# Softplus in a scan-bound kernel: one logarithm with a bias on ScalarE, the rounding term on VectorE, and new orders for all engines

## The chip, the cores and the metric

The kernel runs on one core of one Trainium2 chip. The metric is device time in microseconds (us). The engines are named as the profile names them: PE is TensorE, DVE is VectorE, ACT is ScalarE, POOL is GpSimd, SP is the engine whose queue issues the DMAs.

## The reference

x has the shape (16, 1024, 256) in fp32: 16 sequences of 1024 steps and 256 features. Two feed-forward blocks stand around a state-space block, each with a layer norm ahead of it:

```python
x = x + 0.5 * ffn(layernorm(x))          # silu(x Wg) * (x Wu), then Wd; hidden width 768
x = x + attn(layernorm(x))
x = x + 0.5 * ffn(layernorm(x))

def attn(x):                             # e = 256 features, n = 16 states
    z, params = x @ W_z.T, x @ W_params.T
    dt = softplus(params[..., :64] @ W_dt.T + b_dt)
    u  = silu(causal_conv(x, conv_w))    # 4 taps, one filter for each feature
    A  = -exp(A_log)
    A_tilde = exp(dt * A)
    B_tilde = where(|A| < 1e-5, dt, (A_tilde - 1) / (A + 1e-10))
    h[t] = A_tilde[t-1] * h[t-1] + B_tilde[t-1] * u[t-1]     # for each feature and state
    y  = sum over n of C[t, n] * h[t, e, n]
    return ((y + u * D) * silu(z)) @ W_out.T
```

The step that is changed is the softplus. It is evaluated as max(y, 0) + log(1 + exp(-|y|)), with a correction for the rounding of the sum: with s = 1 + e rounded to fp32 and v = s - 1, the term e - v that the rounding lost is added back.

## The kernel before, in words

The 16 sequences are called rows. Each row has 1024 steps, in two chunks c of 512, and 256 features, in two halves h (or p) of 128 partitions. For each row there are 32 scans (16 states by two halves), each over 128x1024. For each of them:

- ACT makes the decays with an exponential of dt times a coefficient (event `ex`, L1043),
- DVE scans them into the PSUM tensor g_bank (event `scan`, L1282) and multiplies the result by the inverse coefficient and by the row of C (event `cm`, L1318),
- POOL adds that product to acc (also event `cm`, L1122), and the SP queue fetches the next row of C, spread over the partitions.

The first and the last row are cut the other way: their scans are over 128x512, two to a state (one for each half) and chunk, 64 in the row.

Around the scans, and beside them, run the two feed-forward blocks of the neighbouring rows: PE makes the gate and up products (L782) and the down product (L794), ACT takes silu and scales (L925, L933), POOL or DVE multiplies them (L1090, L1235), DVE takes the layer norm's statistics (L1193, L1201) and the residual (L1243). The events `ai` and `aj` (L1254, L1260) start acc on DVE.

The softplus is made for each half and chunk, four times a row and 64 times in all, on tiles of 128x512:

- `da` on ACT: |y| into dt (L1001), max(y, 0) into sp_r (L1004), exp(-|y|) into dt (L1006);
- `dl` on ACT: sp_l = 1 + dt (L1013), sp_v = sp_l - 1 (L1016, the tile that the profile calls odd), sp_l = ln(sp_l) (L1018), each waiting for the one before;
- `dp` on POOL: sp_l - sp_v (L1077), + dt (L1080), + sp_r into dt (L1082).

The order of all work is written out. The tables ROW (rows in the middle), HEAD (row 0), SECOND (row 1), LATE (row 14) and TAIL (row 15) give each event a time in units of one scan; `schedule()` sorts all events by it, and each engine issues its own part of that one list, in order. Each engine is an in-order queue: an instruction whose semaphore isn't there holds up all behind it. Semaphores are counted ahead by the class Counts from the same list. DVE's program stands twice in the kernel, once for inputs with coefficients below 1e-5 and once without; a branch at its start picks the one, and with these inputs it is the short one (one instruction to a scan).

Of the kernel before, what the change touches and what calls it, by code (L numbers as in the profile page):

```python
# [1355 lines left out]
```

## Time and profile before

| | |
|---|---|
| median of 3 runs | 2221.56 us (2221.4 to 2221.57) |
| the profiled execution | 2221.01 us |
| its span in the trace | 2219.1 us |
| granted TensorE clock, mean over the span | 0.977 |

The profile is of one execution; its span runs from the first to the last instruction, and some 1.9 us of its time lie outside. Engine times in it are the unions of the instructions' own times; register, branch and semaphore work isn't counted. A row of a listing by line gives the engine, the operation, what is written <- what is read, the shapes, the count, then the busy time in us and the mean of one in ns, then the idle time of that engine just before these instructions and who ended it. In a listing in order of time the first number is the start and the second the duration, both in us. In a wait of less than 150 ns no releaser is named.

### The profile page before, as it was taken

What the parts mean: (1) busy time and instruction counts of PE and PEld (TensorE: products, weight loads), DVE (VectorE), ACT (ScalarE), POOL (GpSimd) and SP (SyncE); (2) the same over time, 40 slices, a digit from 0 to 9 for tenths busy, and PEclk for the clock granted to TensorE, in tenths of its full rate; (3) what the DMA queues carried; (4) which work ended last, traced back from release to release, by engine and by line L of the source; (5) the groups of instructions that cost most, each with busy time, mean ns of one, the idle gap of its engine ahead of it and who ended that gap; (6) DMA issues with size and microseconds to landing.
All of it is one profiled execution on the core that took longest, in us unless ns stands there. A gap on an engine that the chain in (4) does not pass through costs nothing. (4 is left out here: it accounts for less than half of the span.)

```text
span 2219.1 us, 27781 instructions
## 1 busy us (share of the span) xinstructions
PE 2110.7 (95%) x8708; PEld 1286.0 (58%) x8708; DVE 2088.8 (94%) x2233; ACT 1961.2 (88%) x2946; POOL 1946.3 (88%) x1510
## 2 busy tenths in 40 slices
PE   6995999999999999999999999999999999998578
PEld 3452656566565656656565665656566565656245
DVE  2599999999999999999999999999999999999992
ACT  5988898989999898999989899998989999896882
POOL 2687899899999989999998999999899999998673
PEclk9997999999999999999999999999999999999779
DMA  2122444444444444434444444444444444433120
GB/s 94 44 82 68 141 136 152 152 144 152 135 154 142 151 153 144 152 135 152 143 148 152 149 151 136 152 138 149 152 149 150 140 152 135 152 134 123 63 71 29
DMA packets 112023, 291.14 MB, mean 131 GB/s; under 512 B 11201, under 2 KB 45314, under 8 KB 111874
## 3 DMA queue, kind: packets, MB, share of 16 engines
q1 hardware_dynamic: 111874, 289.35, 39.5%
q8 instruction: 69, 1.13, 0.2%
q14 instruction: 80, 0.66, 0.1%
HBM read 271.49 MB, written 17.83 MB: 130 GB/s over the span
## 5 line engine op out<-in xcount | busy, mean ns | idle before, releaser
L1282 DVE TENSOR_TENSOR_SCAN g_bank<-du_bank,ring 128x1024 f32<-128x1024 f32 (+1 forms) x512 | 1099.8, 2154 | 9.3 <-ACT ring L1043 2.5
L1122 POOL TENSOR_TENSOR acc<-acc,ring 128x1024 f32<-128x1024 f32 x512 | 1023.5, 1999 | 79.9 <-DVE ring L1318 66.7
L794 PE MATMUL work<-wd_t,hid 128*128 128x256 f32 x3072 | 684.8, 380 | 4.3 <-DVE hid L1235 4.2
L1318 DVE SCALAR_TENSOR_TENSOR ring<-g_bank,inv_a,ring 128x1024 f32<-128x1024 f32 (+1 forms) x576 | 661.5, 1154 | 5.3 <-POOL acc L1122 2.5
L794 PEld LDWEIGHTS work<-wd_t,hid 128*128 128x128 f32 x3072 | 582.3, 190 | 116.0 <-issue 20.1
L1043 ACT ACTIVATE ring<-dt,a_coef 128x1024 f32<-128x1024 f32 (+1 forms) x576 | 578.2, 1048 | 1.8 <-POOL dt L1082 0.2
L1090 POOL TENSOR_TENSOR hid<-hid,odd 128x512 f32<-128x512 f32 x320 | 347.4, 1093 | 69.2 <-ACT hid L933 40.5
L782 PE MATMUL work<-xt_hi,wg_t 128*128 128x512 f16 x768 | 296.1, 386 | 20.7 <-ACT odd L925 6.2
L782 PE MATMUL work<-xt_hi,wu_t 128*128 128x512 f16 x768 | 297.0, 387 | 12.8 <-ACT hid L933 4.5
L925 ACT ACTIVATE odd<-work 128x512 f32<-128x512 f32 x384 | 222.0, 606 | 89.1 <-PE work L782 87.3
L782 PE MATMUL work<-xt_lo,wu_t 128*128 128x512 f16 x768 | 296.4, 386 | 0.0
L782 PE MATMUL work<-xt_lo,wg_t 128*128 128x512 f16 x768 | 295.8, 385 | 0.0
L861 ACT ACT_TABLE_LOAD x213 | 273.3, 1283 | 3.8
L833 PE MATMUL work<-xt,tap_diag 128*128 128x512 f32 x512 | 228.1, 592 | 2.7 <-ACT sp_r L1004 1.4
L933 ACT ACTIVATE hid<-work 128x512 f32<-128x512 f32 x320 | 186.7, 593 | 25.0 <-PE work L782 24.7
L833 PEld LDWEIGHTS work<-xt,tap_diag 128*128 128x128 f32 x512 | 96.7, 189 | 121.7 <-issue 114.9
L782 PEld LDWEIGHTS work<-xt_hi,wg_t 128*128 128x128 f16 x768 | 75.8, 99 | 126.2 <-ACT xt_lo L912 13.1
L782 PEld LDWEIGHTS work<-xt_hi,wu_t 128*128 128x128 f16 x768 | 76.0, 99 | 115.2 <-issue 16.6
L782 PEld LDWEIGHTS work<-xt_lo,wu_t 128*128 128x128 f16 x768 | 76.2, 99 | 94.4 <-issue 22.9
L804 PE MATMUL work<-wo_t,acc 128*128 128x256 f32 x512 | 125.5, 390 | 5.4 <-POOL acc L1113 5.3
L782 PEld LDWEIGHTS work<-xt_lo,wg_t 128*128 128x128 f16 x768 | 76.0, 99 | 94.0 <-issue 18.8
L811 PE MATMUL work<-xt,wz_t 128*128 128x512 f32 x256 | 123.8, 606 | 6.0 <-ACT hid L933 3.3
...
## 6 DMA issues: line engine op xcount, KB each, us to landing
...
```

What stands on the lines that cost most here:

```text
L782: last = pe.matmul(dst[:], w[:, k, m * P:(m + 1) * P], part_[:, k, :], start=(k == 0 and i == 0), stop=(k == EH - 1 and i == 1))
L794: last = pe.matmul(dst[:, j * E:(j + 1) * E], hid[:, K.unit[f, bt, c, m] % HIDS, t:t + P], wd_t[:, m, :], start=(m == 0), stop=(m == HM - 1))
L804: last = pe.matmul(dst[:, j * E:(j + 1) * E], acc[bt % 2][:, h, t:t + P], wo_t[:, h, :], start=(h == 0), stop=(h == EH - 1))
L833: last = pe.matmul(dst[:], tap_diag[:, h, k, :], xt[:, h, k + c * CH:k + (c + 1) * CH], start=(k == 0), stop=(k == KW - 1))
L861: nc.scalar.preload_act_table_set(name)
L925: nc.scalar.activation(sil[:, K.at["silu", ev][1] % SILUS, :], bank(job)[:], ACT.Silu, scale=GATE_SCALE).then_inc(freed(job), 1)
L933: nc.scalar.activation(hid[:, K.unit[ev[1:]] % HIDS, :], bank(job)[:], ACT.Copy, scale=H_SCALE).then_inc(freed(job), 1)
L1043: nc.scalar.activation(dst, dt[bt % 2][:, h, t], ACT.Exp, scale=a_coef[:, h, s:s + 1]).then_inc(S["decay"], 1)
L1090: nc.gpsimd.tensor_tensor(v, v, sil[:, k, :], ALU.mult).then_inc(S["product"], 1)
L1122: nc.gpsimd.tensor_tensor(v, v, shaped(bt, cg[:, K.number[ev[1:]] % TERMS, :]), ALU.add).then_inc(S["summed"], 1)
L1282: scan = nc.vector.tensor_tensor_scan(g, du_h, d_h, first[0], ALU.add, ALU.mult)
L1318: nc.vector.scalar_tensor_tensor(v, g, inv_a[:, h, s:s + 1], c_row, ALU.mult, ALU.mult).then_inc(S["weighted"], 1)
```

## The change

ACT's part of `dl` is one instruction in place of three: the logarithm of dt with a per-partition tile of ones as its bias. The rounding term sp_v is made on DVE, by one TENSOR_SCALAR with two additions (+1, then -1), which is a new event on DVE's list with its own semaphore sp_one. POOL's first subtraction waits for both. All five tables of times are new, so the order on every engine is another one.

```diff
 ROW = {
-    "da": [-9.914, -9.105, -4.311, -1.005],
-    "dl": [-9.438, -5.645, -3.692, -0.598],
-    "dp": [-10.06, -4.984, -2.59, -1.097],
+    "da": [-8.362, -8.161, -5.086, -3.146],
+    "dl": [-7.272, -4.465, -2.733, -2.14],
+    "dp": [-7.183, -4.139, -2.053, -1.976],
...
-            return [(one[kind], {"da": 2, "dp": 3, "dl": 3, "Ts": EH}.get(kind, 1))]
+            more = [("sp_one", 1)] if kind == "dl" else []
+            return more + [(one[kind], {"da": 2, "dp": 3, "Ts": EH}.get(kind, 1))]
...
                     wait(act, "sp_exp", ("da", bt, h, c))
                     wait(act, "sp_sum", ("dp", bt, h - 1, c) if h else ("dp", bt - 1, EH - 1, c))
-                    nc.scalar.activation(sp_l[:, c, :], dt[bt % 2][:, h, 1 + c * CH:1 + (c + 1) * CH], ACT.Copy,
-                                         bias=1.0).then_inc(S["sp_ln"], 1)
-                    wait(act, "sp_ln", ev, less=2)
-                    nc.scalar.activation(sp_v[:, c, :], sp_l[:, c, :], ACT.Copy, bias=-1.0).then_inc(S["sp_ln"], 1)
-                    wait(act, "sp_ln", ev, less=1)
-                    nc.scalar.activation(sp_l[:, c, :], sp_l[:, c, :], ACT.Ln).then_inc(S["sp_ln"], 1)
+                    nc.scalar.activation(sp_l[:, c, :], dt[bt % 2][:, h, 1 + c * CH:1 + (c + 1) * CH], ACT.Ln,
+                                         bias=ones[:]).then_inc(S["sp_ln"], 1)
...
                     wait(pool, "sp_ln", ("dl", bt, h, c))
+                    wait(pool, "sp_one", ("dl", bt, h, c))
                     nc.gpsimd.tensor_tensor(sp_l[:, c, :], sp_l[:, c, :], sp_v[:, c, :],
                                             ALU.subtract).then_inc(S["sp_sum"], 1)
...
+                    elif kind == "dl":
+
+                        _, bt, h, c = ev
+                        wait(dve, "sp_exp", ("da", bt, h, c))
+                        wait(dve, "sp_sum", ("dp", bt, h - 1, c) if h else ("dp", bt - 1, EH - 1, c))
+                        nc.vector.tensor_scalar(sp_v[:, c, :], dt[bt % 2][:, h, 1 + c * CH:1 + (c + 1) * CH], 1.0, -1.0,
+                                                ALU.add, ALU.add).then_inc(S["sp_one"], 1)
```

The order shows how DVE's list moves. The first piece is of DVE before, in the last third of a middle row; L1282 is a scan (the listing writes it as SCALAR_TENSOR_TENSOR into g_bank), L1318 the product with C that needs it, and the square brackets name the semaphores that an instruction waits for.

```order
L1282 SCALAR_TENSOR_TENSOR g_bank<-du_bank,ring 128x1024 [waits decay,weighted]
L1254 TENSOR_TENSOR work<-work,u 128x512 [waits u_first,bank_ready0]
L1318 SCALAR_TENSOR_TENSOR ring<-g_bank,inv_a,ring 128x1024 [waits summed,c_spread0,scanned]
L1254 TENSOR_TENSOR work<-work,u 128x512 [waits bank_ready2]
L1282 SCALAR_TENSOR_TENSOR g_bank<-du_bank,ring 128x1024 [waits decay,weighted]
L1260 SCALAR_TENSOR_TENSOR acc<-u,consts,work 128x512 [waits times_u]
L1260 SCALAR_TENSOR_TENSOR acc<-u,consts,work 128x512
L1318 SCALAR_TENSOR_TENSOR ring<-g_bank,inv_a,ring 128x1024 [waits summed,c_spread1,scanned]
L1243 SCALAR_TENSOR_TENSOR x_fin<-work,x_fin 128x512 [waits bank_ready3]
```

The second piece is of DVE after the change, at the same place. The lines have moved: L1290 is the scan, L1326 the product, L1262 the new TENSOR_SCALAR, L1268 the old L1260 and L1244 the old L1243.

```order
L1326 SCALAR_TENSOR_TENSOR ring<-g_bank,inv_a,ring 128x1024 [waits summed,c_spread1,scanned]
L1262 TENSOR_SCALAR odd<-dt 128x512 [waits sp_sum,sp_exp]
L1290 SCALAR_TENSOR_TENSOR g_bank<-du_bank,ring 128x1024 [waits decay,weighted]
L1268 SCALAR_TENSOR_TENSOR acc<-u,consts,work 128x512 [waits times_u]
L1326 SCALAR_TENSOR_TENSOR ring<-g_bank,inv_a,ring 128x1024 [waits summed,c_spread2,scanned]
L1290 SCALAR_TENSOR_TENSOR g_bank<-du_bank,ring 128x1024 [waits decay,weighted]
L1244 SCALAR_TENSOR_TENSOR x_fin<-work,x_fin 128x512 [waits bank_ready0]
L1326 SCALAR_TENSOR_TENSOR ring<-g_bank,inv_a,ring 128x1024 [waits summed,c_spread0,scanned]
L1290 SCALAR_TENSOR_TENSOR g_bank<-du_bank,ring 128x1024 [waits decay,weighted]
L1262 TENSOR_SCALAR odd<-dt 128x512 [waits sp_sum,sp_exp]
L1326 SCALAR_TENSOR_TENSOR ring<-g_bank,inv_a,ring 128x1024 [waits summed,c_spread1,scanned]
```

A middle row now has four L1262 among its 32 scans, each alone between a scan and a product: three behind a scan, one behind a product. The pairs with nothing between them change too: in a middle row before, 5 scans are followed at once by their own product and 14 products at once by the next scan; after, 3 and 11.

On ACT the three instructions of `dl` become one. The first piece is of ACT before, in a middle row (L1043 makes decays):

```order
L1001 ACTIVATE dt<-work 128x512
L1004 ACTIVATE sp_r<-work 128x512
L1006 ACTIVATE dt<-dt 128x512
L1043 ACTIVATE ring<-dt,a_coef 128x1024 x2
L1013 ACTIVATE sp_l<-dt 128x512
L1016 ACTIVATE odd<-sp_l 128x512
L1018 ACTIVATE sp_l<-sp_l 128x512
```

The second is of ACT after, in a middle row (L1005, L1008, L1010 are the old L1001, L1004, L1006; L1017 is the logarithm with its bias):

```order
L1005 ACTIVATE dt<-work 128x512
L1008 ACTIVATE sp_r<-work 128x512
L1010 ACTIVATE dt<-dt 128x512
L1043 ACTIVATE ring<-dt,a_coef 128x1024
L1017 ACTIVATE sp_l<-dt,consts 128x512
```

Over the whole program ACT's list falls from 214 table loads (L861, now L865) to 184.

## Rows read from the trace of the kernel before

**Rows 1.** Part 1 of the page: busy us, share of the span, instructions.

```profile
PE 2110.7 (95%) x8708; PEld 1286.0 (58%) x8708; DVE 2088.8 (94%) x2233; ACT 1961.2 (88%) x2946; POOL 1946.3 (88%) x1510
```

**Rows 2.** Busy time by stretch, cut at rows' first scans (columns: its first line).

```profile
core 0: us, PE busy (x) PEld busy (x) DVE busy (x) ACT busy (x) POOL busy (x), PEclk, DMA share, GB/s
0.00:82.94 82.94, 65.01 (x263) 36.88 (x264) 18.29 (x71) 56.01 (x99) 30.02 (x41) 1.00 0.23 73
82.94:222.12 139.18, 109.39 (x365) 56.12 (x365) 133.15 (x198) 123.97 (x198) 109.88 (x83) 0.90 0.23 71
...
354.13:1910.94 1556.81, 1552.01 (x6530) 956.59 (x6528) 1548.92 (x1538) 1431.76 (x2137) 1457.69 (x1129) 1.00 0.44 147
...
2039.00:2166.64 127.64, 83.78 (x295) 47.63 (x296) 121.96 (x170) 105.07 (x149) 90.01 (x61) 0.76 0.23 70
2166.64:2219.10 52.46, 44.66 (x207) 30.28 (x205) 9.69 (x20) 15.06 (x27) 18.62 (x17) 0.99 0.09 31
```

**Rows 3.** DVE by line, rows 2 to 13: busy us, mean ns, idle before.

```profile
L1282 DVE TENSOR_TENSOR_SCAN g_bank<-du_bank,ring 128x1024 f32<-128x1024 f32 x385 | 880.9, 2288 | 5.8
L1318 DVE SCALAR_TENSOR_TENSOR ring<-g_bank,inv_a,ring 128x1024 f32<-128x1024 f32 x384 | 488.9, 1273 | 2.1
L1193 DVE BATCH_NORM_STATS2 stats<-x_mid 128x6 f32<-128x256 f32 x96 | 39.2, 408 | 0.0
...
L1243 DVE SCALAR_TENSOR_TENSOR x_fin<-work,x_fin 128x512 f32<-128x512 f32 x49 | 33.2, 677 | 0.0
...
L1201 DVE BATCH_NORM_AGGREGATE meanvar<-stats 128x2 f32<-128x6 f32 x288 | 26.4, 155 | 0.0
```

**Rows 4.** DVE in order of time, row 7: start us, duration us.

```profile
1002.77 2.29 DVE L1282 TENSOR_TENSOR_SCAN g_bank<-du_bank,ring 128x1024 f32<-128x1024 f32 x1
1005.09 1.28 DVE L1318 SCALAR_TENSOR_TENSOR ring<-g_bank,inv_a,ring 128x1024 f32<-128x1024 f32 x1
1006.41 2.30 DVE L1282 TENSOR_TENSOR_SCAN g_bank<-du_bank,ring 128x1024 f32<-128x1024 f32 x1
...
1016.05 1.29 DVE L1318 SCALAR_TENSOR_TENSOR ring<-g_bank,inv_a,ring 128x1024 f32<-128x1024 f32 x1
1017.25 0.68 DVE L1235 SCALAR_TENSOR_TENSOR hid<-odd,work 128x512 f32<-128x512 f32 x1
1017.85 2.29 DVE L1282 TENSOR_TENSOR_SCAN g_bank<-du_bank,ring 128x1024 f32<-128x1024 f32 x1
1020.05 0.40 DVE L1193 BATCH_NORM_STATS2 stats<-x_fin 128x6 f32<-128x256 f32 x1
1020.36 1.27 DVE L1318 SCALAR_TENSOR_TENSOR ring<-g_bank,inv_a,ring 128x1024 f32<-128x1024 f32 x1
```

**Rows 5.** DVE's smallest SBUF-to-SBUF groups, whole span.

```profile
L1171 DVE TENSOR_SCALAR part_ident<-ident 128x128 f16<-128x128 f32 x1 | 0.2, 226 | 0.0
...
L1162 DVE TENSOR_SCALAR kept<-tiny 128x32 f32<-128x32 f32 x1 | 0.2, 182 | 0.0
```

**Rows 6.** POOL's groups by line, rows 2 to 13.

```profile
L1122 POOL TENSOR_TENSOR acc<-acc,ring 128x1024 f32<-128x1024 f32 x385 | 769.6, 1999 | 52.4 <-DVE ring L1318 43.1 <-POOL acc L1122 0.9
L1090 POOL TENSOR_TENSOR hid<-hid,odd 128x512 f32<-128x512 f32 x240 | 260.8, 1093 | 10.5 <-ACT hid L933 10.5
...
L1080 POOL TENSOR_TENSOR odd<-sp_l,dt 128x512 f32<-128x512 f32 x48 | 52.5, 1095 | 3.8
...
L1113 POOL TENSOR_TENSOR acc<-acc,odd 128x1024 f32<-128x1024 f32 x24 | 48.0, 1999 | 0.0
```

**Rows 7.** Two of ACT's groups by line, whole span.

```profile
L861 ACT ACT_TABLE_LOAD x213 | 273.3, 1283 | 3.8
...
L1016 ACT ACTIVATE odd<-sp_l 128x512 f32<-128x512 f32 x64 | 40.4, 632 | 2.0
```

**Rows 8.** All engines in order of time, before the first scan.

```profile
77.53 0.63 ACT L1018 ACTIVATE sp_l<-sp_l 128x512 f32<-128x512 f32 x1
...
82.94 1.23 DVE L1282 TENSOR_TENSOR_SCAN g_bank<-du_bank,ring 128x512 f32<-128x512 f32 x1 [0.21 <-ACT ring L1043]
```

More of the change, by code:

```diff
@@ L153 @@
-    "op": [35.06, 36.163, 37.79, 39.377],
-    "rc": [35.575, 36.637, 36.528, 37.925],
-    "ra": [36.686, 37.081, 38.723, 40.428],
[62 rows of a table added]
+    "gate": [22.902, 33.832],
+    "scan": [2.069, 2.861, 3.745, 5.331, 6.972, 8.54, 8.917, 9.446, 10.237, 11.213, 12.305, 13.392, 14.705, 16.607,
+        17.327, 19.066, 19.869, 20.405, 21.329, 21.6, 22.847, 23.595, 24.545, 25.735, 27.009, 27.752, 28.449, 29.234,
+        29.829, 30.713, 32.618, 33.544],
+    "cm": [2.475, 3.732, 5.293, 6.006, 7.925, 8.789, 9.081, 9.751, 10.367, 11.766, 12.502, 14.578, 15.507, 16.878,
+        18.1, 19.134, 20.165, 20.818, 21.522, 22.324, 23.034, 24.127, 25.71, 25.972, 27.116, 28.088, 28.829, 29.566,
+        29.96, 31.503, 32.904, 33.713],
@@ L210 @@
[L210 to L215 removed]
+    "sj1": [-416.545, -399.359, -383.731, -309.346, -259.77, -234.766, -224.568, -206.525],
@@ new lines @@
+    "ln1": [-300.165, -152.578],
+    "lr1": [-217.189, -172.147],
+    "lx1": [-263.701, -147.013],
+    "T1": [-216.593, -95.986],
+    "Te1": [-201.163, -132.221],
+    "Ts1": [-214.325, -82.539],
+    "Tl1": [-192.654, -116.794],
+    "sj2": [-97.203, -95.012, -84.414, -81.252, -23.364, -18.874, -17.593, -16.986],
+    "ln2": [-80.219, -14.269],
+    "lr2": [-53.401, -19.383],
+    "lx2": [-66.256, -12.97],
+    "T2": [-53.486, -5.584],
+    "Te2": [-62.765, -8.441],
+    "ga1": [-209.213, -200.065, -137.254, -98.472, -88.211, -70.776, -72.81, -69.074, -61.766, -61.738, -56.328,
+        -28.093],
@@ new lines @@
+    "dn1": [-66.802, -63.76, -19.221, -17.962],
+    "rs1": [-97.511, -81.18, -27.411, -22.036],
+    "rp": [-78.255, -55.327, -25.504, -25.451],
+    "pm": [-51.651, -5.189],
+    "pe": [-55.742, -4.478],
+    "cw": [-28.111, -3.013],
+    "cv": [-34.106, 1.213, -48.635, 11.32],
+    "us": [-40.893, 3.227, -39.643, 8.84],
+    "z": [16.197, 15.329, -0.006, 16.371],
+    "zs": [12.346, 12.848, 6.559, 18.212],
+    "dt": [-49.921, -0.736, -45.552, 7.04],
+    "da": [-54.127, -3.181, -50.793, 7.492],
@@ new lines @@
+    "dl": [-53.514, 1.324, -43.065, 9.226],
+    "dp": [-49.193, 3.092, -46.694, 8.992],
+    "rm": [-26.762, 4.775, -24.47, 8.913],
+    "ai": [-39.579, 11.469, -35.873, 10.39],
+    "aj": [-36.658, 14.18, -35.797, 11.736],
+    "u0": [-38.941],
+    "dt0": [-38.811],
+    "d": [-41.304, 7.587],
+    "db": [-35.737, 10.134],
+    "gate": [16.924, 33.677],
+    "scan": [-34.028, -30.332, -24.192, -21.131, -12.669, -10.607, -8.982, -6.795, -3.112, -0.993, 0.146, 4.081,
+        4.384, 4.747, 9.566, 10.92, 12.484, 14.917, 15.499, 16.491, 18.184, 20.055, 21.029, 23.235, 23.868, 24.26,
+        26.333, 27.657, 28.693, 28.969, 30.9, 31.904],
@@ new lines @@
+    "Te1": [-85.227, -53.861],
+    "Ts1": [-79.389, -47.402],
+    "Tl1": [-83.712, -50.472],
+    "sj2": [-27.454, -26.946, -26.414, -25.609, -16.662, -15.628, -14.263, -14.127],
+    "ln2": [-21.241, -13.942],
+    "lr2": [-20.1, -12.896],
+    "lx2": [-15.908, -12.768],
+    "T2": [-13.71, -12.475],
+    "Te2": [-15.02, -12.368],
+    "ga1": [-65.443, -55.976, -47.669, -44.736, -41.89, -38.591, -37.859, -34.567, -28.964, -28.785, -27.778,
+        -22.995],
+    "si1": [-71.898, -62.691, -45.971, -48.563, -46.118, -40.471, -41.085, -35.479, -27.739, -24.851, -27.354,
+        -24.194],
@@ new lines @@
+    "up1": [-55.972, -52.12, -45.867, -42.011, -40.268, -37.272, -44.768, -37.612, -33.853, -31.404, -27.389,
+        -18.302],
+    "sc1": [-65.911, -60.842, -49.985, -47.625, -42.45, -47.795, -35.317, -30.637, -32.352, -25.151],
+    "hp1": [-53.927, -44.657, -41.52, -45.734, -41.872, -34.431, -38.55, -25.173, -27.452, -24.818],
+    "sh1": [-39.679, -21.305],
+    "dn1": [-33.884, -31.023, -16.297, -13.854],
+    "rs1": [-35.232, -30.827, -19.282, -14.153],
+    "rp": [-32.402, -28.249, -18.083, -16.296],
@@ new lines @@
+    "pm": [-13.575, -11.07],
+    "pe": [-13.76, -8.204],
+    "cw": [-15.275, -14.049],
+    "cv": [-12.48, -9.462, -5.177, -4.642],
+    "us": [-8.831, -9.408, -5.309, -5.111],
+    "z": [1.568, 6.615, 0.066, 12.303],
+    "zs": [0.357, 6.119, -0.65, 12.334],
+    "dt": [-13.438, -8.327, -7.074, -1.522],
+    "da": [-13.283, -7.794, -6.473, -2.315],
+    "dl": [-12.049, -6.23, -4.261, -2.007],
+    "dp": [-11.989, -6.843, -3.678, -1.765],
+    "rm": [0.171, -4.774, 3.791, -4.26],
+    "ai": [-0.729, -2.577, 2.936, -3.055],
@@ L259 @@
+    "aj": [2.286, 1.5, 3.976, -1.148],
+    "u0": [-2.866],
+    "dt0": [0.808],
 }
 LATE = {
[20 rows of a table removed]
[20 rows of a table added]
 }
 TAIL = {
[19 rows of a table removed]
[L304 to L310 removed]
@@ L317 @@
-    "op": [41.513, 43.467, 110.745, 111.473],
-    "rc": [37.192, 43.796, 102.83, 102.955],
-    "ra": [35.129, 39.708, 111.342, 118.198],
[19 rows of a table added]
+    "gate": [25.544, 91.569],
+    "scan": [1.744, 3.381, 3.72, 5.487, 7.128, 8.771, 13.019, 13.293, 16.026, 17.155, 18.293, 20.077, 20.813, 21.526,
+        23.533, 24.464, 26.624, 31.364, 34.81, 36.513, 37.812, 40.294, 48.785, 51.645, 53.921, 54.754, 58.93, 69.693,
+        71.719, 72.998, 75.231, 81.755],
+    "cm": [2.693, 3.644, 4.563, 6.624, 7.923, 10.402, 13.066, 13.941, 17.06, 17.194, 19.526, 20.371, 21.428, 22.665,
+        23.647, 25.035, 29.386, 32.151, 35.331, 37.189, 38.044, 41.408, 51.235, 53.698, 54.099, 56.924, 66.524, 70.2,
+        72.247, 74.739, 81.13, 85.342],
@@ L320 @@
+    "op": [36.631, 38.424, 112.916, 114.857],
+    "rc": [33.937, 35.654, 96.722, 99.356],
+    "ra": [30.166, 30.868, 101.188, 142.773],
 }
```

119 lines of the change are left out of this document (36 added, 83 removed), and 235 rows, old and new, of tables (LATE, ROW, SECOND, TAIL).

## Prediction

> **What bounds the kernel now.** I read the page's busy shares first, then the busy time by stretch, then the groups of the engine that is fullest, then its instructions in order of time.
>
> The shares alone don't decide: PE 95%, DVE 94%, ACT and POOL 88% [rows 1]. The stretches do. Rows 2 to 13 run from 354.13 to 1910.94, 1556.81 us for 12 rows or 129.73 a row, and in them DVE is busy for 1548.92, so idle for 0.66 us a row. PE shows 1552.01, but ends of matmuls are modelled, so that this number can't tell a full PE from a nearly full one. ACT is idle for 125 us (10.4 a row) and POOL for 99 (8.3 a row) [rows 2].
>
> That DVE sets the period can be added up from its own starts. From a scan to the next instruction it is 2.20 us when something independent follows (1017.85 to 1020.05) and 2.32 when its own product follows at once (1002.77 to 1005.09). From a product it is 1.20 to an independent instruction and 1.32 to the next scan. So a pair with nothing in between costs 0.12 more. An instruction of 128x512 that fills a gap takes 0.60 (1017.25 to 1017.85), BN_STATS 0.31 [rows 4]. A group of four aggregates is 26.4/72 = 0.37 busy, some 0.29 once the overlap of 0.08 with its neighbour is off [rows 3]. A middle row before has 32 scans, 32 products, 19 such bare pairs (5 + 14), 24 BN_STATS, 6 groups of aggregates and 16 instructions of 128x512 (four lines like L1243, which the reader sees with 49 in 12 rows [rows 3]):
>
> 32 x 2.20 + 32 x 1.20 + 19 x 0.12 + 24 x 0.31 + 6 x 0.29 + 16 x 0.60 = 108.8 + 2.3 + 7.4 + 1.7 + 9.6 = 129.8 us.
>
> The measured row is 129.73. DVE has nothing left to give; whatever is added to it lengthens the row, and whatever is taken from ACT there shortens nothing.
>
> **The change part by part.**
>
> *ACT loses work.* Two of three instructions go, 64 times each; one takes 0.63 us [rows 7], and 30 of 214 table loads at 1.28 go with the new order [rows 7]: 128 x 0.63 + 30 x 1.28 = 119 us of ACT. The logarithm's bias becomes a tile; no row here shows what that adds, and with 10 us a row idle even half a microsecond for each of four would stay hidden. In the middle rows I cost all of this at nothing, since DVE covers it. At the head it counts once: the last softplus stands in the chain to the first scan (L1018 at 77.53, first scan at 82.94 [rows 8]); ahead of L1018 go two dependent instructions of 0.63 [rows 7], so -1.3 us. The bounds are 0 and -2.6, for two such groups ahead of the first scan.
>
> *DVE gets 64 TENSOR_SCALARs of 128x512.* No such size is in the trace. The nearest rows of that operation are 182 ns for 32 elements and 226 for 128 [rows 5]: 0.46 ns an element, where one element a cycle costs about 1.0 (677 ns for 512, 408 for 256, hence 1.05 [rows 3]). So it streams two a cycle: 182 + 480 x 0.46 = 403 ns, as long as a BN_STATS of 408, and I take that one's 0.31 to 0.32 from start to start. The other bound is one element a cycle, 677 ns and 0.60. Each fills a gap, and a middle row has 14 bare pairs after (3 + 11) for 19 before: 4 x 0.32 - 5 x 0.12 = +0.68 us a row; by the slow bound 4 x 0.60 - 0.6 = +1.8.
>
> *What the new instruction does beside POOL.* This is the term that decides. No instruction of DVE's in the middle rows takes two elements a cycle out of SBUF; those of before run beside POOL and keep their durations to the nanosecond (677, 736, 408 [rows 3]), and so do POOL's (1999, 1093 [rows 6]). The two TENSOR_SCALARs that the trace has ran during the setup, with POOL idle. So the trace bounds it only from both sides: no wait, or a wait until the POOL instruction under way has ended, at most 2.00 us. If DVE and POOL can't run such a pair together, an arrival at any moment finds POOL busy, and the wait that is left is the sum of squares over twice the time: 385 of 1999 ns, 48 of about the same length (L1113 is one of the two groups), 240 of 1093 and five groups of 48 like L1080 [rows 6]: (433 x 4.0 + 480 x 1.2)/(2 x 1556.8) = 0.74 us. For four a row that is 3.0 us.
>
> I take the wait. The double rate has to use something that the single rate doesn't, and the Trainium skill names it. Its page "SBUF — State Buffer", section "Who interferes with whom", says that VectorE and GpSimd share one pair of SBUF ports, that a tensor_scalar in a two-port mode takes it as an exclusive lock, and that whoever comes second is blocked until the first has ended. "VectorE: DVE Perf Modes", section "Mode 2×_2P", gives that mode to an fp32 tensor_scalar from SBUF to SBUF, as the slope of [rows 5] agrees; that it blocks no row of before shows. By the pages the sum is the one with the wait, by the rows of before alone it is anything from none to the whole. Without these sentences the wait stands as a guess between 0 and 2.00 us, at its mean for a random arrival.
>
> Behind the waiting TENSOR_SCALAR stand, in three of four places, a product L1326, and in the fourth a scan; for the product waits POOL's addition, for both waits ACT's next decay. POOL has 8.3 us a row idle, so it pays nothing for being held for 4 x 0.4.
>
> *The sum.* Of 64 TENSOR_SCALARs two stand ahead of the first scan and 62 between the first and the last, 15.5 rows' worth. Span 2219.1, with 1.9 outside 2221.0. Plus 15.5 x 0.68 = 10.5, plus 62 x 0.74 = 45.9, minus 1.3 at the head, minus 2 for row 0, where DVE is idle for 6.0 of 139.18 us [rows 2] and a third of that may take up its share. 2274.1. The median is 0.5 above the profiled run, so 2274 to 2275.
>
> **The rivals.**
>
> *No wait on POOL.* For it: DVE's and POOL's durations are steady today. Against: none of today's pairs is of this kind. Two elements a cycle: 2221.0 + 10.5 - 1.3 = 2230. One a cycle: 2221.0 + 15.5 x 1.8 - 1.3 = 2248.
>
> *Ends that pay for it (the other side).* The orders of row 0 and of the last row are new, and there DVE has room: 82.94 us before the first scan with 18.29 busy, 6.0 idle in row 0, 5.7 of 127.64 in the last row, and 52.46 us behind the last scan [rows 2]. Less ACT work could let those rows run at DVE's pace: -1.3 and one table load of 1.3 at the head, -6.0 and -5.7 in the rows, together -14.3. With the TENSOR_SCALARs at 0.32 and no wait: 2221.0 + 10.5 - 14.3 = 2217. It decides from 10.5 us on and is a gain to be measured from 15. Against it: 129.8 against 129.73 says that 12 rows can't give anything, and behind the last scan PE, with 44.66 busy of 52.46, has as many products left as before.
>
> *A stall on semaphores.* In DVE's in-order list the TENSOR_SCALAR waits for ACT's exponential and, for the second half, for POOL's three additions of the first (3 x 1.09 behind up to 2.00 [rows 6]). Some 15 us of DVE work lie between the two, so I give it little. If each came 0.5 to 1 us early: 2221.0 + 10.5 + 31 to 62 = 2262 to 2294. It would show as idle time before the instruction, the wait on POOL as a long instruction or as idle time without a semaphore.
>
> **How the numbers follow.** The wait on POOL 0.50 (four fixed phases a row, each 0 to 2.0, so their mean scatters: 2255 to 2295 by itself); no such wait 0.26, 2228 to 2248; the stall 0.06; ends that pay and more, 0.11, 2205 to 2217; ends that pay just so, 0.07. Less than 0.2% (4.4 us) can't be told from no change here. So slower 0.82, the same 0.07, faster 0.11. The predicted time is that of the first case, 2274. The range reaches down over the no-wait case to 2224 and up to 2298, where most of the first case ends; every TENSOR_SCALAR waiting for the whole of a long addition would be 2221.0 + 10.5 + 124 = 2355, which I leave out.
>
> **What would show it.** Right: a row of 133.4 us in the middle (129.73 now), DVE still idle for less than 1 us of it apart from what stands before L1262, L1262 with a mean near 1.1 us or with idle time before it, its times spread from 0.4 to 2.4; ACT idle for some 20 us a row, POOL for about 10. The scans at 2288 ns and the products at 1273 as before. Wrong: L1262 at 0.40 or 0.68 without spread, and rows of 130.4 or 131.5. Quite wrong: rows under 129.7, since then DVE didn't set them; or a gain at the ends, to be seen as a first scan before 80 us and less than 50 us behind the last one.

## The result, and the profile after

The changed kernel takes 2247.66 us (median of 3 runs, 2245.72 to 2249.33), where the kernel before takes 2221.56: a ratio of 1.0116, with a 95% interval of 1.0102 to 1.013. It is slower by 26 us; the forecast was 53. The profiled execution took 2247.66 us with a span of 2245.9.

First the page's busy shares, the line that answers to [rows 1]:

```profile
PE 2117.9 (94%) x8708; PEld 1277.0 (57%) x8708; DVE 2126.4 (95%) x2297; ACT 1856.5 (83%) x2788; POOL 1954.7 (87%) x1510
```

DVE has 37.6 us more, ACT 104.7 less, POOL 8.4 more although it runs the same 1510 instructions. Then the busy time by stretch, cut at the rows' first scans as in [rows 2]:

```profile
0.00:76.54 76.54, 58.79 (x230) 31.08 (x230) 19.68 (x74) 50.67 (x89) 28.99 (x40) 0.98 0.25 79
76.54:213.80 137.26, 112.88 (x399) 61.78 (x398) 134.21 (x202) 123.41 (x195) 112.06 (x84) 0.95 0.24 74
346.97:1937.70 1590.73, 1564.29 (x6530) 951.70 (x6529) 1578.77 (x1585) 1353.36 (x2017) 1464.56 (x1129) 1.00 0.43 144
2068.50:2196.20 127.70, 84.70 (x306) 48.78 (x307) 122.75 (x172) 94.64 (x140) 92.28 (x63) 0.79 0.23 70
2196.20:2245.87 49.67, 42.25 (x195) 28.41 (x193) 9.62 (x20) 14.29 (x25) 16.10 (x15) 0.98 0.10 32
```

Against [rows 2], stretch by stretch: before the first scan 76.54 for 82.94 (-6.4; the scan itself starts at 76.46), row 0 137.3 for 139.2 (-1.9), rows 2 to 13 1590.7 for 1556.8 (+33.9), the last row the same to 0.1, and 49.7 behind the last scan for 52.5 (-2.8); rows 1 and 14 make up the other +3.9. A middle row takes 132.56 on average for 129.73. The ends gave back some 11 us, and the middle took 38.

DVE by line in rows 2 to 13, beside [rows 3]:

```profile
L1290 DVE TENSOR_TENSOR_SCAN g_bank<-du_bank,ring 128x1024 f32<-128x1024 f32 x384 | 879.5, 2290 | 6.7 <-ACT du_bank L1025 1.9
L1326 DVE SCALAR_TENSOR_TENSOR ring<-g_bank,inv_a,ring 128x1024 f32<-128x1024 f32 x384 | 488.9, 1273 | 5.2 <-DMA ring<-c_rows 3.5 <-POOL acc L1123 0.5
...
L1262 DVE TENSOR_SCALAR odd<-dt 128x512 f32<-128x512 f32 x48 | 38.6, 805 | 0.0
```

Scans and products last as long as before. The new L1262 has a mean of 805 ns and no idle time before it, so no semaphore holds it up. All 64 of them, the answer for the one line over the whole span:

```profile
L1262 DVE TENSOR_SCALAR odd<-dt x64: 410/460/1925, 62.4 to 2052.1; 128x512 f32<-128x512 f32 x64
```

The shortest takes 410 ns, the median 460, the longest 1925. What the long ones have in common is on POOL. DVE in order of time in row 5, and POOL beside it:

```profile
832.58 2.27 DVE L1290 TENSOR_TENSOR_SCAN g_bank<-du_bank,ring 128x1024 f32<-128x1024 f32 x1
834.75 1.88 DVE L1262 TENSOR_SCALAR odd<-dt 128x512 f32<-128x512 f32 x1
836.55 1.27 DVE L1326 SCALAR_TENSOR_TENSOR ring<-g_bank,inv_a,ring 128x1024 f32<-128x1024 f32 x1
...
845.80 0.42 DVE L1262 TENSOR_SCALAR odd<-dt 128x512 f32<-128x512 f32 x1
846.13 2.29 DVE L1290 TENSOR_TENSOR_SCAN g_bank<-du_bank,ring 128x1024 f32<-128x1024 f32 x1
```

```profile
834.35 2.00 POOL L1123 TENSOR_TENSOR acc<-acc,ring 128x1024 f32<-128x1024 f32 x1
836.77 1.09 POOL L1078 TENSOR_TENSOR sp_l<-sp_l,odd 128x512 f32<-128x512 f32 x1 [0.43 <-DVE odd L1262]
...
844.26 1.09 POOL L1091 TENSOR_TENSOR hid<-hid,odd 128x512 f32<-128x512 f32 x1
845.96 2.11 POOL L1123 TENSOR_TENSOR acc<-acc,ring 128x1024 f32<-128x1024 f32 x1 [0.61 <-DVE ring L1326]
```

At 834.75 POOL is 0.40 into an addition that ends at 836.34; L1262 ends 0.28 later, at 836.63. At 845.80 POOL has finished at 845.35 and stands waiting for the product, so L1262 takes 0.42; the addition that starts 0.16 behind it takes 2.11 in place of 2.00. In the middle rows this repeats to within 0.05 us: 1.88, 0.42, 0.50 and 0.41 us, where 0.33 from start to start is what one costs without a wait. The waits are 1.47, 0, 0.09 and 0, or 1.56 us a row.

The row's 2.69 us (132.42 in row 5, less 129.73) add up on DVE: 4 x 0.33 = 1.32 for the instruction, 1.56 for the waits, -0.6 for five bare pairs fewer, and 0.38 for one thing the prediction hadn't, together 2.66. These are ACT, and then DVE, in order of time in row 5:

```profile
805.63 2.07 ACT L878 ACTIVATE normed<-x_fin,affine 128x256 f32<-128x256 f32 x4
807.60 1.01 ACT L1025 ACTIVATE du_bank<-du 128x1024 f32<-128x1024 f32 x1
```

```profile
807.93 0.43 DVE L1194 BATCH_NORM_STATS2 stats<-x_mid 128x6 f32<-128x256 f32 x1
808.64 2.30 DVE L1290 TENSOR_TENSOR_SCAN g_bank<-du_bank,ring 128x1024 f32<-128x1024 f32 x1 [0.28 <-ACT du_bank L1025]
```

In the new order ACT's copy of the carries stands behind four scalings, and in row 5 a scan starts 0.71 behind a BN_STATS where 0.33 is usual. This wait is not the same in every row, and it has a partner that the rows of before don't have either: the product 8 us into the row waits for its row of C. DVE at the two places in row 7, and then in row 3:

```profile
1017.93 2.30 DVE L1290 TENSOR_TENSOR_SCAN g_bank<-du_bank,ring 128x1024 f32<-128x1024 f32 x1
1020.26 1.29 DVE L1326 SCALAR_TENSOR_TENSOR ring<-g_bank,inv_a,ring 128x1024 f32<-128x1024 f32 x1
...
1072.99 0.42 DVE L1194 BATCH_NORM_STATS2 stats<-x_mid 128x6 f32<-128x256 f32 x1
1073.77 2.30 DVE L1290 TENSOR_TENSOR_SCAN g_bank<-du_bank,ring 128x1024 f32<-128x1024 f32 x1 [0.36 <-ACT du_bank L1025]
```

```profile
487.73 2.30 DVE L1290 TENSOR_TENSOR_SCAN g_bank<-du_bank,ring 128x1024 f32<-128x1024 f32 x1
490.75 1.28 DVE L1326 SCALAR_TENSOR_TENSOR ring<-g_bank,inv_a,ring 128x1024 f32<-128x1024 f32 x1 [0.72 <-DMA ring<-c_rows]
...
543.47 0.42 DVE L1194 BATCH_NORM_STATS2 stats<-x_mid 128x6 f32<-128x256 f32 x1
543.80 2.28 DVE L1290 TENSOR_TENSOR_SCAN g_bank<-du_bank,ring 128x1024 f32<-128x1024 f32 x1
```

From the scan to its product it is 2.33 in row 7 and 3.02 in row 3, from BN_STATS to the scan 0.78 and 0.33: where one waits, the other doesn't. In eight of the 12 rows the two come to 3.11 or 3.12 together, 0.45 more than the 2.66 that they take without a wait, and those rows are 132.41 to 132.45 long. In the three rows where the product waits longer than 0.45, the row is longer as well (132.67 to 133.25). So between these two places DVE has 0.45 us to spare, and another path sets the time. In row 5 it starts with POOL's acc, which releases PE at 749.02. From there PE shows no gap up to the work that ACT waits for at 804.66, and ACT's scalings and its copy follow without a wait. PE's first instruction there, and its busy time in that stretch (length, busy time, instructions, granted clock, DMA):

```profile
749.02 1.13 PE L808 MATMUL work<-wo_t,acc 128*128 128x256 f32 x4 [0.22 <-POOL acc L1114]
```

```profile
749.10:804.60 55.50, 55.50 (x252) 1.00 0.46 152
```

The ends of matmuls are modelled, so the second line says only that PE has no wait there that the profile can show.

### The profile page after: what moved, and what is told of

It reads as the page before. It is cut to its first block and busy times, and to the rows that moved or that the text cites. A ratio compares the mean times of both kernels' runs of the same rounds, so it can differ in the third digit from the quotient of the medians.

```text
span 2245.9 us, 27796 instructions
## 1 busy us (share of the span) xinstructions
PE 2117.9 (94%) x8708; PEld 1277.0 (57%) x8708; DVE 2126.4 (95%) x2297; ACT 1856.5 (83%) x2788; POOL 1954.7 (87%) x1510
## 5 line engine op out<-in xcount | busy, mean ns | idle before, releaser
L1290 DVE TENSOR_TENSOR_SCAN g_bank<-du_bank,ring 128x1024 f32<-128x1024 f32 (+1 forms) x512 | 1101.1, 2157 | 10.7 <-ACT du_bank L1025 3.6
L1326 DVE SCALAR_TENSOR_TENSOR ring<-g_bank,inv_a,ring 128x1024 f32<-128x1024 f32 (+1 forms) x576 | 662.0, 1156 | 6.4 <-DMA ring<-c_rows 3.5
L1043 ACT ACTIVATE ring<-dt,a_coef 128x1024 f32<-128x1024 f32 (+1 forms) x576 | 573.5, 1046 | 3.1 <-DVE g_bank L1290 1.7
```

Of the source, the lines that this page charges most:

```text
L1043: nc.scalar.activation(dst, dt[bt % 2][:, h, t], ACT.Exp, scale=a_coef[:, h, s:s + 1]).then_inc(S["decay"], 1)
L1290: scan = nc.vector.tensor_tensor_scan(g, du_h, d_h, first[0], ALU.add, ALU.mult)
L1326: nc.vector.scalar_tensor_tensor(v, g, inv_a[:, h, s:s + 1], c_row, ALU.mult, ALU.mult).then_inc(S["weighted"], 1)
```

## The experiments

All times are medians of 4 runs, beside before on the same chip (2221.94 to 2222.03). The changed kernel's own ratio, 1.0116, is what theirs are held against. "A row" is a middle row, from first scan to first scan.

### The TENSOR_SCALAR left out, and old code in the new orders

`e1_no_ones` leaves sp_v out: nothing writes it, and POOL subtracts another tile of the same size.

```diff
-                    wait(pool, "sp_one", ("dl", bt, h, c))
-                    nc.gpsimd.tensor_tensor(sp_l[:, c, :], sp_l[:, c, :], sp_v[:, c, :],
+                    nc.gpsimd.tensor_tensor(sp_l[:, c, :], sp_l[:, c, :], sp_r[:, c, :],
...
-                        nc.vector.tensor_scalar(sp_v[:, c, :], dt[bt % 2][:, h, 1 + c * CH:1 + (c + 1) * CH], 1.0, -1.0,
-                                                ALU.add, ALU.add).then_inc(S["sp_one"], 1)
```

> The changed kernel without its TENSOR_SCALAR on DVE (left out: the rounded sum less one; POOL subtracts sp_r in its place, at the same cost). In the changed kernel a middle row is 132.42 us, and the four TENSOR_SCALARs of it take 0.33 us each from start to start when nothing holds them, 1.56 more of waiting for POOL's instruction under way, and fill four gaps of 0.12. Theory 1 (the TENSOR_SCALARs and their wait are the whole cost; the new orders cost nothing): row 132.42 - 1.32 - 1.56 + 0.50 = 130.0, total 2248 - 15.5 x 2.4 = 2211. Rival (the new orders themselves stall DVE, PE or the C rows' transfers): the row stays at 131 or more, total 2225 or more.

2233.63 us, a ratio of 1.0052 (1.0035 to 1.0069); a row takes 131.59. DVE by line in rows 2 to 13:

```profile
L1281 DVE TENSOR_TENSOR_SCAN g_bank<-du_bank,ring 128x1024 f32<-128x1024 f32 x384 | 878.6, 2288 | 7.1 <-ACT du_bank L1024 1.8
L1317 DVE SCALAR_TENSOR_TENSOR ring<-g_bank,inv_a,ring 128x1024 f32<-128x1024 f32 x384 | 488.3, 1272 | 21.4 <-POOL acc L1121 15.6 <-DMA ring<-c_rows 2.5
```

Without its fourfold instruction DVE catches up with POOL, and a product waits 1.3 us once a row for POOL's acc. In row 5 that product is this one:

```profile
850.70 1.28 DVE L1317 SCALAR_TENSOR_TENSOR ring<-g_bank,inv_a,ring 128x1024 f32<-128x1024 f32 x1 [1.22 <-POOL acc L1121]
```

So 2.4 us of DVE (1.32 and 1.56 less, four bare pairs more) bring back only 0.83 of a row, and 1.86 of the 2.69 are there without any TENSOR_SCALAR: 1.2 at that product, 0.3 in two shorter waits behind it, and the 0.45 at the two places of above, less 0.12 for one bare pair fewer than before. Of the 26 us, 14 go with the instruction, and 12 are there without it. The new orders are longer by themselves.

`e2_old_code_new_orders` has the old ACT code of three instructions, no TENSOR_SCALAR, and the new tables.

```diff
-                    nc.scalar.activation(sp_l[:, c, :], dt[bt % 2][:, h, 1 + c * CH:1 + (c + 1) * CH], ACT.Ln,
-                                         bias=ones[:]).then_inc(S["sp_ln"], 1)
+                    nc.scalar.activation(sp_l[:, c, :], dt[bt % 2][:, h, 1 + c * CH:1 + (c + 1) * CH], ACT.Copy,
+                                         bias=1.0).then_inc(S["sp_ln"], 1)
+                    ...
+                    nc.scalar.activation(sp_v[:, c, :], sp_l[:, c, :], ACT.Copy, bias=-1.0).then_inc(S["sp_ln"], 1)
+                    ...
+                    nc.scalar.activation(sp_l[:, c, :], sp_l[:, c, :], ACT.Ln).then_inc(S["sp_ln"], 1)
```

> The code of before (three instructions of dl on ACT, none on DVE) with the five new tables. Theory 1: DVE's list is that of e1_no_ones, ACT has 5 us a row more and 19.5 idle to take it, so the row is 130.0 and the total 2211 to 2213, under the kernel before: the new tables' ends (first scan 6.4 us earlier, 2.8 us less behind the last scan, row 0 1.8 shorter) are a gain that the TENSOR_SCALARs ate. Rival (the ends gained because ACT had less to do, not by the order): total 2219 to 2225, first scan at 80 us or later.

A miss: 2287.28 us, 1.0293 (1.0276 to 1.031), a row 134.94. DVE by line, in its middle rows:

```profile
L1321 DVE SCALAR_TENSOR_TENSOR ring<-g_bank,inv_a,ring 128x1024 f32<-128x1024 f32 x383 | 487.1, 1272 | 28.3 <-POOL acc L1125 23.4 <-DMA ring<-c_rows 2.5
...
L1238 DVE SCALAR_TENSOR_TENSOR hid<-odd,work 128x512 f32<-128x512 f32 x47 | 31.8, 678 | 27.4 <-ACT odd L928 27.4
```

The new orders count on the lighter ACT: with the old one DVE waits for ACT's silu and for POOL. The lighter ACT is thus worth nothing in the old orders by the count of the prediction, and 3.35 us a row (134.94 against e1's 131.59) in the new. The first scan of e2 is at 78.7, where before has it at 82.9, e1 at 77.3 and the changed kernel at 76.5: of the 6.5 us that the changed kernel gained at the head, some 4.3 come with the order, and 1.4 to 2.2 with the lighter softplus.

### What makes the TENSOR_SCALAR wait

`e4_single_rate` keeps the instruction in its place but has it write a sum as well; it then copies dt + 0, so the rounding term is left out.

```diff
-                        nc.vector.tensor_scalar(sp_v[:, c, :], dt[bt % 2][:, h, 1 + c * CH:1 + (c + 1) * CH], 1.0, -1.0,
-                                                ALU.add, ALU.add).then_inc(S["sp_one"], 1)
+                        nc.vector.tensor_scalar(sp_v[:, c, :], dt[bt % 2][:, h, 1 + c * CH:1 + (c + 1) * CH], 0.0, None,
+                                                ALU.add, ALU.add, accum_out=consts[:, FLAG + 1:FLAG + 2]).then_inc(S["sp_one"], 1)
```

> The changed kernel with the TENSOR_SCALAR in a form that also sums its output (it copies dt with 0 added in place of the rounded sum less one, and the sum goes to an unused column). If that form goes at one element a cycle and Theory 1 is about the double rate alone, each takes 0.60 us from start to start wherever it stands and never waits for POOL: row 132.42 - 1.56 - 1.32 + 2.4 = 131.9, total 2240, a little more if the sum costs an instruction of its own. Rival A (every SBUF-to-SBUF TENSOR_SCALAR waits for POOL, whatever its rate): the first of a row takes 2.1 to 2.2 us, total 2265. Rival B (the form keeps the double rate and waits): as the changed kernel, 2248.

2236.93 us, 1.0068 (1.0051 to 1.0085), a row 131.76. DVE by line in rows 2 to 13:

```profile
L1262 DVE TENSOR_SCALAR_CACHE_REDUCE odd<-dt 128x512 f32<-128x512 f32 x48 | 32.4, 675 | 0.0
...
L1262 DVE DVE_READ_ACCUMULATOR odd<-dt 128x1 f32 x48 | 3.9, 82 | 0.0
```

A form that streams half as fast makes a faster kernel. The first of row 5 starts at 830.95, again 0.405 us after the start of a POOL addition of 2.00, the very phase of 834.75 above, and takes 0.675. By DVE's account the row is 129.73 + 4 x 0.60 - 0.6 = 131.53, and the other 0.23 are at the two places of above. So it is this form of the instruction that waits, not its place in the list, its semaphores or its operands.

`e5_two_inputs` computes the same term with a SCALAR_TENSOR_TENSOR, one of whose inputs is a column of ones spread over the row.

```diff
+                        nc.vector.scalar_tensor_tensor(sp_v[:, c, :], dt[bt % 2][:, h, 1 + c * CH:1 + (c + 1) * CH], 1.0,
+                                                       ones.to_broadcast([P, CH]), ALU.add,
+                                                       ALU.subtract).then_inc(S["sp_one"], 1)
```

> The changed kernel with the TENSOR_SCALAR as SCALAR_TENSOR_TENSOR: (dt + 1) - a tile of ones, spread by a step of zero, the same numbers. It has two inputs in SBUF, which no instruction of DVE's in the middle rows has, and can't go at the double rate. e4_single_rate's four instructions took 0.60 us each without a wait (row 131.76, total 2237). Theory 1 (only the double rate meets POOL): the same here, row 131.8, total 2237. Rival (a second input out of SBUF also goes the way that POOL goes): the first of a row, which starts 0.4 us into a POOL addition of 2.0, takes 0.68 + 1.6 us, row 133.3, total 2260.

2262.19 us, 1.0181 (1.0164 to 1.0198), a row 133.47. DVE in order of time, and POOL:

```profile
975.77 2.13 DVE L1262 SCALAR_TENSOR_TENSOR odd<-dt,consts 128x512 f32<-128x512 f32 x1
977.82 1.28 DVE L1327 SCALAR_TENSOR_TENSOR ring<-g_bank,inv_a,ring 128x1024 f32<-128x1024 f32 x1
```

```profile
975.36 2.00 POOL L1123 TENSOR_TENSOR acc<-acc,ring 128x1024 f32<-128x1024 f32 x1
```

It waits like the TENSOR_SCALAR, and ends 0.54 after POOL's end at 977.36, since it needs longer itself. Waiting isn't bound to two elements a cycle; two inputs from SBUF at one element a cycle (0.67 us where nothing holds it) do it too. DVE's instructions of 677 ns [rows 3], and L1260 with a mean of 736 in the same rows of before, read one of their inputs from PSUM (the tile work), and don't wait. The Trainium skill, "SBUF — State Buffer", section "Who interferes with whom", has both cases: two SBUF inputs contend with a GpSimd instruction that reads SBUF, and the form of tensor_scalar that writes its sum does not. This trace and e4's agree, with 2.13 us here and 0.675 there in the same phase.

`e3_moved` puts the first TENSOR_SCALAR of a row, from row 2 on, behind the next product in place of the scan; the other three stay.

```diff
+                    elif kind == "dl" and ev[2:] == (0, 0) and ev[1] >= 2:
+                        later.append(ev)
...
+                        while later:
+                            made_one(later.pop())
```

> The changed kernel with only the first TENSOR_SCALAR of rows 2 to 15 set one gap later on DVE, right behind the next product, for whose addition POOL stands waiting. Theory 1 (it waits for the POOL instruction under way): its duration falls from 1.88 to 0.42 us, the addition behind it takes 2.11 in place of 2.00, the bare pairs stay as many, so a row loses 1.4 and the total is 2248 - 14 x 1.45 = 2227. Rival (it is long for a reason of its own data or semaphores, such as the exponential or the additions of POOL before it): it stays near 1.9 us or shows idle time, total 2243 or more.

2240.82 us, 1.008 (1.0063 to 1.0097), a row 131.80. DVE in order of time shows the moved one:

```profile
833.74 1.29 DVE L1332 SCALAR_TENSOR_TENSOR ring<-g_bank,inv_a,ring 128x1024 f32<-128x1024 f32 x1
834.94 0.55 DVE L1228 TENSOR_SCALAR odd<-dt 128x512 f32<-128x512 f32 x1
835.40 2.29 DVE L1296 TENSOR_TENSOR_SCAN g_bank<-du_bank,ring 128x1024 f32<-128x1024 f32 x1
```

Its wait falls from 1.47 to 0.14, but the second one, at 843.34, now comes 0.23 us into a POOL product and takes 1.15: it waits 0.74 where it waited for nothing. Of 1.33 us saved, 0.6 stay, so the mechanism of its forecast held and its 2227 did not. `e9_all_moved` does the same to all four (the edit is against e3).

```diff
-                    elif kind == "dl" and ev[2:] == (0, 0) and ev[1] >= 2:
+                    elif kind == "dl" and ev[1] >= 2:
```

> All four TENSOR_SCALARs of the rows from 2 on stand one gap later on VectorE, behind the next product in place of the next scan; nothing else moves. Theory A (the phase between VectorE and GpSimd that each gap finds is what it pays, and behind a product a gap is worth some 0.48 us on average, as the trace of the changed kernel gives if every gap behind a product is asked how long GpSimd's instruction under way still ran): 4 x 0.48 = 1.9 us a row where the row pays 1.56 now, so about 2247 to 2254 us, with one or two of the four at 0.41 to 0.45 us and the wait gathered in the others. Theory B (behind a product GpSimd's addition is only released, so the TENSOR_SCALAR always goes first and waits for nothing, as the one at 845.80 of the changed kernel): all four at 0.40 to 0.45 us, -1.56 us a row in 14 rows, so 2226 us.

2266.28 us, 1.0198 (1.0181 to 1.0215), a row 133.75. The waits are as theory A had them, 0.13, 0, 0.68 and 0.84, together 1.65; but the kernel is slower than A's range. DVE by line, rows 2 to 13:

```profile
L1332 DVE SCALAR_TENSOR_TENSOR ring<-g_bank,inv_a,ring 128x1024 f32<-128x1024 f32 x384 | 487.9, 1271 | 19.1 <-POOL acc L1123 14.9 <-DMA ring<-c_rows 1.9
L1228 DVE TENSOR_SCALAR odd<-dt 128x512 f32<-128x512 f32 x48 | 39.7, 827 | 0.0
```

A product waits 1.2 us a row for acc, 108 us into the row, and it is the one that waits in e1. POOL's softplus isn't later than in the changed kernel (in row 5 its first two parts start 92.0 and 104.5 us into the row for 92.2 and 105.0): DVE, which no longer stands 1.47 behind an earlier scan, is there sooner than POOL. The same group with nearly the same mean duration (827 for 805) goes with a row that is 1.3 us longer.

`e6_on_pool` gives the instruction to POOL, ahead of its subtraction.

```diff
+                    nc.gpsimd.tensor_scalar(sp_v[:, c, :], y, 1.0, -1.0, ALU.add, ALU.add).then_inc(S["sp_one"], 1)
```

> The changed kernel with the TENSOR_SCALAR on POOL, ahead of its first subtraction. DVE's list is then that of e1_no_ones (row 131.59, of which DVE stands 1.3 us before a product until POOL's addition before last is done). Theory 2 (in the new orders POOL's softplus group is what DVE catches up with, so each us put into it comes out of the row): four instructions of some 1.1 us make the row 132.7 (one of them counts) to 136 (all four), total 2250 to 2290. Rival (POOL's 9.4 us of idle time a row take them): row 131.6, total 2234.

2363.37 us, 1.0634 (1.0616 to 1.0651), a row 139.95. POOL's group, and DVE's products, over the whole span:

```profile
L1077 POOL TENSOR_SCALAR odd<-dt 128x512 f32<-128x512 f32 x64 | 123.7, 1932 | 6.2 <-ACT sp_l L1017 6.2
```

```profile
L1320 DVE SCALAR_TENSOR_TENSOR ring<-g_bank,inv_a,ring 128x1024 f32<-128x1024 f32 (+1 forms) x576 | 661.9, 1155 | 139.2 <-POOL acc L1124 133.0 <-DMA ring<-c_rows 3.7
```

The expectation had taken 1.1 us for one, and it takes 1.93. Four of them are 7.7 us, the row is 8.4 longer than e1's, and DVE stands 133 us for POOL's acc: POOL's 9.5 us of idle time a row in e1 hide none of it.

### Slack for POOL, and ACT's copy put first

If DVE meets POOL's acc, a third buffer for products should help. Two kernels take it from the ring of decays: `e7_no_ones_three_products` (e1 with it) and `e8_three_products` (the changed kernel with it).

```diff
-DECAYS = 5
-TERMS = 2
+DECAYS = 4
+TERMS = 3
```

> e1_no_ones with three buffers for the products in place of two and four for the decays in place of five (SBUF is full). Theory 2 (e1 stands at POOL's addition before last, because two buffers let DVE run only so far ahead): the 1.3 us wait is gone, row 130.2, total 2214 or a little over; what the TENSOR_SCALARs cost is then 2.2 us a row and not the 0.8 that e1 shows. Rival (the wait is a matter of the order on POOL, whatever the buffers, or four decays hold ACT back): row 131.5 or more, total 2232 or more.

> The changed kernel with three buffers for the products and four for the decays. There DVE hardly stands for POOL (0.75 us idle a row in all), so by Theory 1 (single rate of scans plus the TENSOR_SCALARs' own time and wait) nothing changes but the moments at which they meet POOL: row 131 to 133.5, the first one's wait following what POOL is at. Rival (POOL's lag is in the row in another form, as the stretched scans and statistics are): row under 131.

2314.49 us, 1.0416 (1.0398 to 1.0433), and 2321.37 us, 1.0445 (1.0428 to 1.0463). Neither tells what it was made for. ACT by line in e8, over the whole span:

```profile
L1043 ACT ACTIVATE ring<-dt,a_coef 128x1024 f32<-128x1024 f32 (+1 forms) x576 | 577.3, 1048 | 90.8 <-DVE g_bank L1290 89.5
```

Four decays in the ring are too few: ACT waits 89.5 us for scans to free one (3.1 in all before decays in the changed kernel), and its other work comes late. No product waits for acc any more, but other waits outweigh that. The two lie only 6.9 us apart, and their median middle row is the same to 0.01, 137.23 and 137.24, although L1262 in e8 still has its long wait (at 998.64 it takes 1.88 us): there the whole of the TENSOR_SCALAR is hidden, because something else is late.

`e10_copy_first` moves ACT's copy ahead of the four scalings; `e11_single_rate_copy_first` does so in e4.

```diff
-    "db": [1.434, 18.411],
+    "db": [1.434, 18.295],
```

> One number of the table ROW is changed, so that ScalarE's copy of the scans' carries (du_bank) is issued ahead of the four scalings of the layer norm (normed) and not behind them; the TENSOR_SCALARs stay. Theory A (the 0.38 us that a scan waits once a row for that copy is a term of the row of its own): -0.38 us in 14 rows = -5.3, so 2242 us, and that scan starts without idle time before it. Theory B (the wait is one that VectorE would meet elsewhere, since it catches up with GpSimd or ScalarE at the next place, or the scalings are now late): no gain, 2247 us or more, with the 0.38 us turning up ahead of another scan or product.

> The two edits together: VectorE's added instruction in the form that also writes a sum and copies dt + 0 (no rounding term, streams one element a cycle), and the copy of the carries issued ahead of the four scalings. The first alone gave 2236.93 us. Theory A (terms of a row that add up): 2236.9 - 5.3 = 2231.6 us, row 131.4. Theory B (without the waits on GpSimd VectorE has gained on it already, so it meets another wait instead): 2235 us or more, with idle time of VectorE ahead of a product that waits for GpSimd's acc.

2248.17 us, 1.0121 (1.0104 to 1.0137), and 2247.9 us, 1.0116 (1.0099 to 1.0133). Theory B both times: e10 gains nothing, and e11 is 11 us slower than e4 alone. The wait for the copy is gone (4.5 us of idle time before 384 scans for 6.7, and the copy no longer named), and DVE has others. In e10 a row is 129.92 us plus the time from the scan 8 us into it to its product (2.33 to 3.22), in 11 of 12 rows: what that product waits, mostly for its row of C, now counts in full, and waits of 0.11 and 0.16 have come ahead of L1236. In e11 that wait is longer. DVE in order of time:

```profile
862.04 1.28 DVE L1326 SCALAR_TENSOR_TENSOR ring<-g_bank,inv_a,ring 128x1024 f32<-128x1024 f32 x1
863.84 0.69 DVE L1236 SCALAR_TENSOR_TENSOR hid<-odd,work 128x512 f32<-128x512 f32 x1 [0.52 <-ACT odd L929]
```

Where it comes from stands 50 us earlier. ACT, and PE, of e11 in order of time:

```profile
807.97 1.03 ACT L1025 ACTIVATE du_bank<-du 128x1024 f32<-128x1024 f32 x1 [0.77 <-DVE g_bank L1290]
808.93 2.06 ACT L878 ACTIVATE normed<-x_fin,affine 128x256 f32<-128x256 f32 x4
...
814.31 0.60 ACT L929 ACTIVATE odd<-work 128x512 f32<-128x512 f32 x1
```

```profile
814.97 0.39 PE L786 MATMUL work<-xt_hi,wu_t 128*128 128x512 f16 x1 [1.40 <-ACT odd L929]
```

And PE of e4 at the same place:

```profile
808.80 0.39 PE L786 MATMUL work<-xt_hi,wu_t 128*128 128x512 f16 x1 [0.50 <-ACT odd L929]
```

The copy can't start before a scan has read the old carries, so ACT stands for 0.77 us, and with the copy's own 1.03 all behind it comes late. PE waits 1.40 for ACT in place of 0.50. PE has nothing to catch up with: counted from the row's first scan, its instructions in e11 lag those of e4 by 0.2 us before this place and by 1.1 for the next 50, until ACT's silu, which needs PE's product, is 0.5 us late for DVE. PE by line, rows 2 to 13, for e4 and then for e11:

```profile
L786 PE MATMUL work<-xt_hi,wu_t 128*128 128x512 f16 x576 | 218.6, 380 | 6.4 <-ACT odd L929 6.3
```

```profile
L786 PE MATMUL work<-xt_hi,wu_t 128*128 128x512 f16 x576 | 218.6, 380 | 18.8 <-ACT odd L929 18.6
```

So DVE isn't alone: in the new orders a second path through PE and ACT runs within half a microsecond of it, and sets the first half of a row in the changed kernel; a third runs through POOL's acc.

## Why the prediction was right in its sign and wrong in its size

**DVE sets the row.** Right of the row before as an account, but PE was as close: its records leave 0.40 us of that row idle, less than DVE's 0.66 [rows 2]. The prediction put it aside since the ends of matmuls are modelled, and no run here tells how much room PE had. For the changed list the step holds only in part: DVE has 1.0 us a row idle for 0.7 before, 0.45 us of each row are set by the path through PE, and work taken from DVE comes back as a wait (e1: 2.4 us taken, 0.83 gained; e3: 1.33 and 0.6; e10: the copy's wait and nothing).

**ACT's loss in the middle is worth nothing.** Right in the sum: ACT's idle time went from 10.4 to 19.8 us a row, and no middle row got shorter. e2 qualifies it: the new orders need the lighter ACT.

**The TENSOR_SCALAR by itself.** 403 ns and 0.32 from start to start were predicted, 410 and 0.33 measured, with five bare pairs fewer. The term 4 x 0.32 - 0.6 = 0.68 a row is 0.72 in the trace.

**The wait for POOL.** The mechanism is as predicted, and shown: L1262 has times from 0.41 to 1.93 us, no semaphore before it, ends 0.28 after POOL's instruction, and the same instruction in a form that streams one element a cycle doesn't wait in the same phase (e4). The rule of the Trainium skill ("SBUF — State Buffer", section "Who interferes with whom") thus held where the rows of before showed nothing of it, with 1.47 us of wait at 834.75.

**Its size is the step that failed.** "Its mean for a random arrival", 62 x 0.74 = 45.9, is the term that was mis-sized: 62 of them waited 0.37 on average, 22.7 us in all, and 0.39 in the middle rows. Two things are in the gap of 23. The smaller is a fault of the formula: it takes all that is left of POOL's instruction as wait, but the first 0.13 us lie beside it. The third of a row (856.60) finds 0.22 us left and pays 0.09, the fourth (861.00) finds 0.05 and pays nothing. With 0.13 taken off, the same formula gives 0.63 by my estimate, 7 us less. The larger is that a mean stood for four fixed numbers. A gap finds POOL in nearly the same phase in each middle row, and three of four found it idle or about to end. The text said that the mean of four fixed phases scatters and kept them in its bounds, but it took the mean for the value, and the bounds of the case, 2255 to 2295, lie above what came. The trace of before wouldn't have given the four: at its own gaps in rows 2 to 13 POOL's instruction ran on for 0.90 us on average behind a scan and 0.53 behind a product, which makes 2.8 us a row for three and one of them, where the forecast had 3.0 and 1.56 came. The phases belong to the new order.

**The ends.** -1.3 was forecast for the head, -6.4 measured, the larger part of it from the new order (e2); and -2.8 behind the last scan, where nothing was forecast. The rival "ends that pay" asked 14.3 us of the ends, in other proportions, and 11 came; it fell because the middle rows took 38.

**What was missing.** The two waits in the first half of a row: 0.33 for the row of C and 0.25 for the copy on average over rows 2 to 13, 0.58 a row. In these rows 43.7 us were forecast and 33.9 came: 16.6 less wait on POOL (18.9 for 35.5), 7.0 for the two waits, and 0.5 for the instruction's 0.72 in place of 0.68 make 34.6 of it. In the rest 9.4 were forecast and -7.1 came: 6.6 less wait, 5.1 at the head and 2.8 behind the last scan, and 2 us that aren't assigned. So of the 26 us between the forecast and the result some 23 are the wait, and the ends and the missing waits nearly cancel, which is luck. This is an account of where time lies. It isn't a list of what each would give back, as e1, e3 and e10 show.

**The other rivals.** No wait on POOL is refuted by L1262's durations; its other case, one element a cycle without a wait, is what e4 is: 2248 was the forecast and 2236.93 came, since head, row 0 and tail gave some 12 us where it had 1.3. No stall on semaphores stood before L1262 after the head (0.0 us idle). The predicted row of 133.4 was 132.4 to 132.6, the predicted mean of 1.1 us was 0.81, ACT's 20 and POOL's 10 us of idle time came true.

**What stays open.** Whether the new instructions in the old orders would be slower: no kernel here has them. By the lists, not by a run, the fourth TENSOR_SCALAR would there wait for a chain that itself waits for work behind it on DVE, so it would need a new place at least. The 1.86 us a row that the orders cost without any TENSOR_SCALAR are placed (e1), but which of the moved events makes POOL's acc and PE late is not shown. No kernel here beats the one before: the best of the new orders is e1's 2233.63, and that one subtracts another tile in place of sp_v, so that what it computes isn't the softplus.
